# Layer 1's turn in another order on VectorE, TensorE and ScalarE

## The reference

```
logits = leaky_relu(a_src[src] + a_dst[dst], 0.2)
ex = exp(logits - segment_max(logits, dst)[dst])
alpha = ex / (segment_sum(ex, dst)[dst] + 1e-16)
out = segment_sum(x[src] * alpha, dst).mean(heads) + bias
```

## Time and profile before

| | us |
|---|---|
| median of 3 runs | 8767.18 (8765.54 to 8771.23) |
| profiled execution | 8752.71 |
| its span | 8751.0 |
| PE busy | 6087.3 (70%) |
| DVE busy | 5776.1 (66%) |
| ACT busy | 3928.5 (45%) |
| POOL busy | 6087.9 (70%) |

### The profile page before, as it was taken

The page is one execution under the profiler, slowest core; times in us unless marked ns, Lnnn a source line. Parts: engine busy times, 40 slices in busy tenths (PEclk is TensorE's granted clock), DMA queues, the critical chain, the costliest instruction groups (busy, mean ns, idle before and its releaser), DMA issues.

```text
span 8751.0 us, 204204 instructions
## 1 busy us (share of the span) xinstructions
PE 6087.3 (70%) x46823; PEld 4733.0 (54%) x46824; DVE 5776.1 (66%) x13889; ACT 3928.5 (45%) x10077; POOL 6087.9 (70%) x6281
## 2 busy tenths in 40 slices
PE   6777777777777777775466666666666666666667
PEld 5656666666666666564344444444444444444446
DVE  5555555555555555555577777777777777777777
ACT  4444444444444445443344444444444444444443
POOL 4777777777777777774777767677676767766650
PEclk8888888888888888886799999898998989899898
DMA  3111111111111111112111111111111111111110
GB/s 100 40 40 40 40 40 40 40 40 40 40 40 40 40 40 40 40 40 37 30 30 29 28 27 27 27 27 28 26 28 27 27 27 28 28 27 27 27 22 15
DMA packets 276883, 301.80 MB, mean 34 GB/s; under 512 B 169511, under 2 KB 173108, under 8 KB 276566
## 3 DMA queue, kind: packets, MB, share of 16 engines
q0 software_dynamic: 200704, 265.33, 16.2%
q1 hardware_dynamic: 74082, 32.92, 1.5%
q10 hardware_dynamic: 2068, 3.20, 0.1%
HBM read 286.33 MB, written 16.30 MB: 35 GB/s over the span
## 4 chain that ended last, share of the span: by engine, by line
POOL 31%; issue 23%; DVE 21%; PE 14%; DVEq 4%; ACTq 2%; POOLq 2%; ACT 2%; DMA 0%; SPq 0%
POOL big L406 31%; PE ps L993 6%; DVE S L509 6%; PE pu L979 4%; DVE state L709 2%; POOLq L397 2%; DVE rowA L658 1%; DVE rel L506 1%; DVE rowD L663 1%; DVE Y L690 1%; DVEq L725 1%; ACT ST L1197 1%; DVE zz L730 1%; ACTq L258 1%; DVE mnew L750 1%
## 5 line engine op out<-in xcount | busy, mean ns | idle before, releaser
L406 POOL DMA_INDIRECT big<-x_dram,idx x3136 | 3095.8, 987 | 1365.6 <-issue 975.3
L406 POOL DMA_INDIRECT big<-q_dram,idx x3136 | 2991.0, 954 | 1041.6 <-issue 1041.6
L979 PE MATMUL pu<-Y,S 128*128 128x265 f32 x7856 | 2142.9, 417 | 739.7 <-DVE Y L690 734.7
L979 PEld LDWEIGHTS pu<-Y,S 128*128 128x128 f32 x7856 | 1494.8, 200 | 1031.4 <-issue 783.5
L690 DVE TENSOR_TENSOR Y<-big,ps 128x1040 f32<-128x1040 f32 x982 | 1210.7, 1233 | 658.6 <-ACT ps L1201 572.4
L509 DVE TENSOR_TENSOR S<-ps,rel 128x1024 f32 x978 | 1197.8, 1225 | 222.1 <-DVE rel L506 222.1
L1098 ACT COPY ST<-ps 128x512 bf16<-128x512 bf16 x978 | 537.5, 585 | 1489.0 <-PE ps L871 1489.0
L885 PE MATMUL pu<-rowX,S 128*128 128x192 bf16 x3936 | 587.5, 285 | 852.5 <-SPq L330 679.3
L546 DVE TENSOR_TENSOR Y<-Y,rowX 128x512 f32<-128x512 f32 x491 | 340.6, 694 | 1143.4 <-ACT rowX L1110 1139.8
L885 PEld LDWEIGHTS pu<-rowX,S 128*128 x3936 | 395.7, 102 | 1011.6 <-issue 922.0
L993 PE MATMUL ps<-identb,S 128*128 128x128 bf16 x3912 | 550.0, 231 | 526.1 <-DVE S L509 524.4
(11 more groups left out here) (176 smaller groups left out, 8465.6 us busy)
## 6 DMA issues: line engine op xcount, KB each, us to landing
big<-q_dram,idx POOLq DMA_INDIRECT x3136
big<-x_dram,idx POOLq DMA_INDIRECT x3136
rowD<-dst_dram SPq DMA_DIRECT2D x196, 32.0 KB
x_dram<-big SPq DMA_DIRECT2D x7, 483.0 KB, 6.2
idx<-srcT_dram SPq DMA_DIRECT2D x98, 32.0 KB, 1.8
dstc<-dstT_dram SPq DMA_DIRECT2D x98, 32.0 KB
q_dram<-state SPq DMA_DIRECT2D x2, 1536.0 KB, 9.6
out<-big SPq DMA_DIRECT2D x6, 448.0 KB
```

What stands on the lines that cost most here:

```text
L406: nc.gpsimd.indirect_dma_start(o, None, x_dram if l else q_dram, bass.IndirectOffsetOnAxis(ap=idx[:, half, t:t + 1], axis=0)).then_inc(gat ...
L979: last = t_.matmul(bank, Sf[:, t, :], Y[:, t, :], start=(t == 0), stop=(t == 7))
```

## The change

The order inside a turn is new on three engines.

- VectorE, turn n: first half of weigh (n-2); the ends' chain (n-3) alone; second half of weigh (n-2); L764 and then the addition L709, now both for n-3; the edges' chain (n-1) alone; `onehot` (n) last.
- TensorE: sums 0 (n-2); destination products, now of n-1 instead of n; sums 1 (n-2); transposes of S (n) last. It keeps the block of the turn before in a register of its own.
- ScalarE: copy of ST, now of n-1 instead of n, first; L1184, L1186, L1190 (n-3); ends 0 (n-1); exp (n-1), now with a wait for `dw` written out; ends 1, now of n-1 instead of n-2.
- The lags of sts, ad, sf1 and acc in `LAGS` follow, and the bank ps[0] is cleared once before the layer. No instruction of a turn is added or taken away.

The diff, cut to its core:

```
-                {"rel": 0, "S": 0, "stp": 0, "sts": 0, "ad": 0, "adx": 1, "zz": 1,
-                 "lz": 1, "dw": 1, "w": 1, "sf0": 1, "sf1": 2, ... "old": 3, "acc": 4}]
+                {"rel": 0, "S": 0, "stp": 0, "sts": 1, "ad": 1, "adx": 1, "zz": 1,
+                 "lz": 1, "dw": 1, "w": 1, "sf0": 1, "sf1": 1, ... "old": 3, "acc": 3}]
...
+            link(v.memset(ps[0][:, :], 0.0))
...
 VectorE, turn1, behind weigh(k, 0, at):
-                    if k.has(4):
-                        ab = acc[:, ds(blocks1.back(4 - t), 1), :, :].rearrange("p b h d -> p (b h) d")
-                        k.after("old", 4)
-                        k.after("tm", 4)
+                    if k.has(3):
+                        ... nz, nl, np, mnew, dd of turn n-3, one behind the other ...
+                    if k.has(2):
+                        weigh(k, 1, at)
+                    if k.has(3):
+                        ab = acc[:, ds(b, 1), :, :].rearrange("p b h d -> p (b h) d")
+                        k.after("e", 3)
+                        v.tensor_tensor(ab, ab, ee[:, 0, :]..., ALU.mult).then_inc(m["old"], 1)
+                        k.after("old", 3)
+                        k.after("tm", 3)
                         v.tensor_tensor(ab, ab, Tm[:, :, :], ALU.add).then_inc(m["acc"], 1)
                     if k.has(1):
                         ... adx, zz, lz, dw of turn n-1, one behind the other ...
                     if k.has(0):
                         k.after("sf1", 2)
                         onehot(k, half, (k.sn % 2) * TG)
-                    if k.has(2):
-                        weigh(k, 1, at)
-                    if k.has(3):
-                        ... the scaling of ab ...
...
 TensorE, turn:
+            pe_blocks = Past(pe, "pe_block", 1, NB - 1)
                 if k.has(2):
                     k.after("tm", 4)
                     sums(k, 0)
+                if k.has(1):
+                    dests = adp[:, ds(pe_blocks.back(1 - max(k.tail, 0)), 1), :, :]...
+                    k.after("adx", 2)
+                    k.after("sts", 1)
+                    for t in range(TG):
+                        last = t_.matmul(ps[2][...], ST[:, t, :], dests, start=True, stop=True)
+                    last.then_inc(L[1]["ad"], 1)
+                if k.has(2):
+                    sums(k, 1)
                 if k.has(0):
                     k.after("S", 0)
-                    k.after("sts", 1)
                     ... the 8 transposes of S ...
-                if k.has(2):
-                    sums(k, 1)
-                if k.has(0):
-                    ... the same products for turn n, behind k.after("adx", 1), k.after("sts", 0) ...
+                    pe_blocks.push(k.b)
...
 ScalarE, turn:
-                    if k.has(2):
-                        ends(k, 1, 2)
+                    if k.has(1):
+                        k.after("stp", 1)
+                        a_.copy(ST[:, :, :], ps[0]...).then_inc(m["sts"], 1)
                     if k.has(3):
                         ... e, mb, tm of turn n-3 ...
                     if k.has(1):
-                        ends(k, 0, 1)
-                    if k.has(0):
-                        k.after("stp", 0)
-                        a_.copy(ST[:, :, :], ps[0]...).then_inc(m["sts"], 1)
-                    if k.has(1):
+                        ends(k, 0)
+                        k.after("dw", 1)
                         k.after("y1", 2)
                         a_.activation(wb[:, :, :], dw[:, :, :], ACT.Exp).then_inc(m["w"], 1)
+                        ends(k, 1)
```

More of the change, by code:

```diff
@@ L703, in turn @@
                         weigh(k, 0, at)
-                    if k.has(4):
-                        ab = acc[:, ds(blocks1.back(4 - t), 1), :, :].rearrange("p b h d -> p (b h) d")
-                        k.after("old", 4)
-                        k.after("tm", 4)
+                    if k.has(3):
+                        b = blocks1.back(3 - t)
+                        mb = Mx[:, ds(b, 1), :]
+                        ends = pu[:, ds(((k.sn + 1) % 2) * 512, YW)]
+                        k.after("U1", 3)
+                        v.tensor_tensor(nz[:, 0:1, :], ends[:, UW:UW + H].unsqueeze(1), adst[:, ds(b, 1), :],
+                                        ALU.add).then_inc(m["nz"], 1)
+                        k.after("nz", 3)
+                        v.scalar_tensor_tensor(nz[:, 1, :], nz[:, 0, :], 0.2, nz[:, 0, :], ALU.mult, ALU.max
+                                               ).then_inc(m["nl"], 1)
+                        k.after("nl", 3)
+                        v.scalar_tensor_tensor(nz[:, 2, :], ends[:, UW + H:YW].to_broadcast([P, H]), -BIG,
+                                               nz[:, 1, :], ALU.add, ALU.add).then_inc(m["np"], 1)
+                        k.after("np", 3)
+                        v.tensor_tensor(mnew[:, :].unsqueeze(1), nz[:, 2:3, :], mb, ALU.max
+                                        ).then_inc(m["mnew"], 1)
+                        k.after("mnew", 3)
+                        v.tensor_tensor(dd[:, 0:1, :], mb, mnew[:, :].unsqueeze(1), ALU.subtract)
+                        v.tensor_tensor(dd[:, 1, :], nz[:, 2, :], mnew[:, :], ALU.subtract).then_inc(m["dd"], 1)
+                    if k.has(2):
[3 more added lines that the diff above has]
+                        k.after("e", 3)
+                        v.tensor_tensor(ab, ab, ee[:, 0, :].unsqueeze(2).to_broadcast([P, H, D + 1]), ALU.mult
+                                        ).then_inc(m["old"], 1)
+                        k.after("old", 3)
+                        k.after("tm", 3)
                         v.tensor_tensor(ab, ab, Tm[:, :, :], ALU.add).then_inc(m["acc"], 1)
@@ L731, in turn @@
                                         ).then_inc(m["zz"], 1)
[L732 to L736, removed]
                         k.after("zz", 1)
@@ L739, in turn @@
                                                ALU.mult, ALU.max).then_inc(m["lz"], 1)
[L740 to L745, removed]
                         k.after("lz", 1)
                         v.tensor_tensor(dw[:, :, :], lz[:, 0], lz[:, 1], ALU.subtract).then_inc(m["dw"], 1)
[L748 to L754, removed]
                     if k.has(0):
@@ L986, in turn @@
                     sums(k, 0)
+                if k.has(1):
+                    dests = adp[:, ds(pe_blocks.back(1 - max(k.tail, 0)), 1), :, :].rearrange("p b k h -> p (b k h)")
+                    k.after("adx", 2)
+                    k.after("sts", 1)
+                    for t in range(TG):
+                        last = t_.matmul(ps[2][:, t * 3 * H:(t + 1) * 3 * H], ST[:, t, :], dests,
+                                         start=True, stop=True)
+                    last.then_inc(L[1]["ad"], 1)
+                if k.has(2):
+                    sums(k, 1)
                 if k.has(0):
                     k.after("S", 0)
-                    k.after("sts", 1)
                     o = ps[0][:, :].bitcast(bf16)
@@ L1162, in _, with ends @@
                             ).then_inc(tab1["tc"], 1)
-            act_tiles = Past(act, "act_tile", 2, 2 * TS - TG)
+            act_tiles = Past(act, "act_tile", 1, 2 * TS - TG)
             act_blocks = Past(act, "act_block", 3, NB - 1)
-            def ends(k, h, back):
-                k.after(f"U{h}", back + 1)
-                at = act_tiles.back(back - max(k.tail, 0))
+            def ends(k, h):
+                k.after(f"U{h}", 2)
+                at = act_tiles.back(1 - max(k.tail, 0))
                 a_.copy(Y[:, h * 4:h * 4 + 4, UW:YW], edgeE[:, ds(at + h * 4, 4), :])
-                a_.copy(Sf[:, h * 4:h * 4 + 4, :], S[:, ds(((k.sn + back) % 2) * TG + 4 * h, 4), :]
+                a_.copy(Sf[:, h * 4:h * 4 + 4, :], S[:, ds(((k.sn + 1) % 2) * TG + 4 * h, 4), :]
                         ).then_inc(L[1][f"sf{h}"], 1)
@@ L1178, in turn @@
                 def turn(k):
-                    if k.has(2):
-                        ends(k, 1, 2)
+                    if k.has(1):
+                        k.after("stp", 1)
+                        a_.copy(ST[:, :, :], ps[0][:, :].bitcast(bf16).rearrange("p (t n) -> p t n", t=TG)
+                                ).then_inc(m["sts"], 1)
                     if k.has(3):
```

9 lines of the change are left out of this document (2 added, 7 removed).

## The result

| | before | after |
|---|---|---|
| median (4 runs each), us | 8766.36 (8754.11 to 8771.23) | 9499.75 (9495.54 to 9516.03) |
| ratio, 95% interval | | 1.0842 [1.0824, 1.0861] |
| profiled execution, span, us | 8752.71, 8751.0 | 9496.01, 9494.3 |

The forecast was 8950 with a range up to 9090. The direction was right; 550 us of the 733 are missing from it.

A forecast was written before the change was run, and what follows sets the result against it. The prediction took a chain of waits as the bound: one-hot, transposes, ScalarE's copy, exp, weighing. Its terms, +175 -53 +54 +13 = +189 us on 8752.7, gave 8942, 8956 as a median; it forecast 8950, range 8670 to 9090.

The forecast's parts named there:

- the sum: 343 turns with a seam +175, 97 without -53, super-group starts +54, ends +13: together +189 us.
- The seam: VectorE at a new group, one-hot's start to next first weighing: 2.2 us (1.85 to 2.6), 1.06 of it uncovered.
- the ends' chain: VectorE, L725 to the second weighing, each instruction waiting for the one before: 1.14 us (0.95 to 1.35).
- the edges' chain: VectorE, start of reduction L717 to start of the one-hot, the chain running alone: 1.65 us.
- the other steps: VectorE: first weighing to ends' logits 1.16, second weighing to scaling 1.14, scaling to adding 0.50, adding to reduction 0.34 us.
- a stall that the sum counts: VectorE's reduction waits for TensorE's products at each super-group's start: 1.2 us stall, 49 x 1.1 = +54 us.
- Rival (a): No VectorE seam shows: 440 turns of 7.07 us, 8592; decides from about 1.7 us downwards (turns 7.5); 9 in 100.
- Rival (b): Splitting VectorE's chains costs nothing, by the page's rule: both kinds of turn 0.66 us shorter, 8632 us; 5 in 100.
- TensorE and ScalarE in such a turn: In turns with a seam, TensorE's products come at T + 5.1, VectorE asks at T + 5.25: 0.15 us spare, nothing added.
- Rival (c): TensorE's seam or added register puts the products half a microsecond behind T + 5.25: +170 us, 9125; 10 in 100.
- The terms for the start (+54) and the end (+13) of a super-group: Start: reduction stalls for products, +54 us; end: scan L658 comes later on VectorE, +0.26 each, +13 us.

The follow-up runs named there:

- run 5: Kernel after, with TensorE's destination products ahead of the first sums and 8 unread matmuls (fillers) behind the transposes: 8945.39 us, 1.0206.
- run 4: Kernel before, with VectorE's edges' chain and then ends' chain instead of laced, plus 8 unread TensorE matmuls ahead of the transposes: 9243.48 us, 1.0551.
- run 6: Kernel after with unread TensorE matmuls, two versions: 8 behind the transposes and 4 ahead (heavier), 9254.74 us; 4 behind alone (lighter), 9191.57 us.
- run 7: Kernel of run 5, with VectorE's scaling L764 behind the one-hot again and the addition of Tm back behind the first weighing: 8772.59 us, 1.0015.
- runs 3 and 4: The first of the two: kernel before, with VectorE's edges' chain and then ends' chain instead of laced, nothing else moved: 9469.8 us, 1.0816.
- run 2: Kernel after, with TensorE's destination products ahead of the first half of the sums instead of behind it: 9289.18 us, 1.0550.

## Why the prediction was wrong

**What held.** The wait for the exp went, VectorE itself was next, and its order costs +189 us in run 5, the very number of the sum. The seam is 2.00 to 2.14 us in the turns shown (2.2 taken); the ends' chain 1.14 (1.14); the edges' chain 1.76 to 1.82 (1.65, of which the 0.16 from the last subtraction to rel stood in no row; it is 0.24); the other steps within 0.05. The errors offset each other, and a stall that the sum counts is absent from run 5, so the equal total is partly luck. Rival (a) is out, by 392 idle times at L691; its own bound was off too, as a seam of 1.7 us would give turns of 7.63, not 7.5, and no gain. Rival (b) is out by the chains' own steps and by run 4: one and the same list of VectorE's instructions, laced and not, differs by 1.0 us a turn at a kept clock, of which 0.2 is the address that comes into the open. In the timeline after that answers to the earlier trace rows, the instructions of the ends' chain start 0.19 to 0.31 us apart where one instruction needs the other, and 0.08 apart where it doesn't (L722 and L723). That contradicts here what "VectorE: DVE Perf Modes" of the Trainium skill says in "The DRAIN you can't avoid", that a semaphore after each operation costs nothing extra. It was measured there on eight copies; no run here repeats that.

**What failed: "TensorE and ScalarE in such a turn".** It left 0.15 us to spare and concluded that "nothing is added". Both ends of that comparison were off. TensorE's sums start 3.16 us behind the one-hot's end (6501.20 to 6504.36), not 2.7: its idle time at the seam is 1.90, where 1.3 was taken over from the old order, in which the last work of the turn stood in TensorE's queue beforehand instead of being waited for. VectorE asks for the products at T + 5.10 (T being the one-hot's end), not 5.25, since its seam is shorter. So the reduction waits 0.34 even in an undisturbed turn. Over all turns run 6 leaves at most 242 us for it. The stall at the start of a super-group was nearly right: 1.36 us in the one looked at (6451.96), 1.2 forecast.

The larger part was not a term of the sum at all: the sums were priced at 2.05 us in every turn. They take 3.90 in many, at 1.2 GHz, behind gaps of 1.28 and 1.90 us in an undisturbed turn where the old order had 1.03 and 1.26; and with the products behind them VectorE waits for all of it, up to 2.23. At least 302 us. Rival (c), "TensorE takes over", had the late products, and less than a third of what was missing: +170 on the sum, 9125, where 544 were missing. It counted a later start and not a slower engine. The earlier trace rows had shown the 3.90 us after a long idle time. It was read as a property of the super-group's start.

**The account:** 189 (VectorE's order) + at most 242 (products behind the sums) + at least 302 (clock) = 733. No run separates the last two further: in run 6 the lighter fillers hold the clock only in part, and the heavier ones hold TensorE up. An estimate: in three turns of the lighter run at the full clock the reduction waits 0.33, 0.36 and 0.39 us; 343 x 0.36 is some 120 us, and 48 or 49 starts of 1.36 some 65, so that more than 302 us are likely the clock's. The terms for the start (+54) and the end (+13) of a super-group weren't isolated. Why the clock falls in one turn and not in the next of the same order stays open too.

## What to carry to other kernels

When one wait is removed, try the smallest edit that removes it: the exchange of two ScalarE instructions alone gave -2.5%, and the larger reordering around it lost that and 8.4% more. Price an engine that nobody waited for anew when its result moves onto the path: with its own seam in the new order, and, where a turn gets longer and TensorE idles more in it, with its work at both clock levels. In a loop like this one, don't end the body with an instruction that waits for its own engine; put work that is ready behind it (run 7).

## What the runs showed of the hardware

- The end of one loop and the start of the next costs VectorE 2.0 to 2.2 us from start to start of the instructions around it (2.07 on average after) and TensorE 1.9 us of idle time, close to layer 0's 1.96; with an instruction of 0.42 us in it, it was 2.19 on average (run 7).
- VectorE instructions on 4 elements a partition that need one another start 0.19 to 0.31 us apart (6503.32 and 6503.63 are the widest), two that don't 0.08; and two chains laced cost 1.0 us a turn less than one behind the other (runs 3 and 4).
- Added matmuls made a kernel faster: 8 fillers (1.95 to 2.00 us in all) took 233 us off the split chains and some 350 off run 2 (235 at the least), with a granted clock of 0.93 instead of 0.83 and 0.76.
